# A gated cross-attention stack on one core: in the third and fifth layers the output transposes and the output projection are issued one round later, and in the third the next queries and keys ahead of the scores

## The reference

```python
# third layer ("l1x"): 16 heads of 8, queries from x, keys and values from ctx
q = (query @ Wq.T + bq) * 8 ** -0.5
k, v = key @ Wk.T + bk, key @ Wv.T + bv
scores = einsum('bhtd,bhsd->bhts', qh, kh) + add_mask
out = einsum('bhts,bhsd->bhtd', softmax(scores), vh)
return out @ Wo.T + bo
# fifth layer ("l2x"): RMS norm of x and ctx, 4 query heads of 32 over one key head, rope, mask
q, k = rope(xn @ q_w) * 32 ** -0.5, rope(mn @ kv_w[0])
enc = softmax(where(mask, q @ k.T, MASK_FILL)) @ (mn @ kv_w[1])
return enc @ out_w
```

## Time and profile before

| what | value |
|---|---|
| median of 3 runs (4495.56 to 4502.85) | 4499.69 us |
| the profiled execution's own time | 4495.28 us |
| its span | 4493.3 us |
| TensorE busy | 3848.1 us, 86% of the span |
| VectorE busy | 2983.7 us, 66% |
| ScalarE busy | 1953.3 us, 43% |
| GpSimd busy | 884.4 us, 20% |
| mean granted TensorE clock, as a share of 2.4 GHz | 0.863 |
| chain that ended last | PE 56%, DVE 20%, SPq 8%, issue 8% |
| third layer | about 1376 to 1925 us from the span's start |
| fifth layer | about 2882 to 3255 us |

### The profile page before, as it was taken

One profiled execution on the slowest core, in us unless ns is written; L12 is line 12 of the kernel. 1 busy time (PEld: TensorE's weight loads), 2 busy tenths in 40 slices (PEclk: granted clock), 3 DMA queues, 4 the chain that ended last, 5 costly groups with the idle time before them and its releaser, 6 DMA issues.

```text
span 4493.3 us, 111186 instructions
## 1 busy us (share of the span) xinstructions
PE 3848.1 (86%) x38938; PEld 3008.1 (67%) x38938; DVE 2983.7 (66%) x9018; ACT 1953.3 (43%) x5436; POOL 884.4 (20%) x639
## 2 busy tenths in 40 slices
PE   5999978888886888889999999877845899999965
PEld 4777745555554556589999999755545767777754
DVE  4666657777765777766666666699972266666669
ACT  3666645655552434333333333222212355555521
POOL 1222223333330000010111111100062032222211
PEclk9999977777776767789999999988757999999976
DMA  3000010000001000000000000100004400000000
GB/s 130 8 7 8 7 23 6 6 6 6 6 7 68 15 16 15 14 6 0 0 0 0 0 0 3 43 11 11 8 22 166 147 13 12 12 12 12 10 13 26
DMA packets 102378, 98.15 MB, mean 22 GB/s; under 512 B 31728, under 2 KB 91120, under 8 KB 101616
## 3 DMA queue, kind: packets, MB, share of 16 engines
q1 hardware_dynamic: 97728, 77.99, 5.8%
q0 software_dynamic: 4096, 8.40, 0.6%
q10 hardware_dynamic: 432, 10.19, 0.6%
HBM read 48.02 MB, written 19.66 MB: 15 GB/s over the span
## 4 chain that ended last, share of the span: by engine, by line
PE 56%; DVE 20%; SPq 8%; issue 8%; POOL 3%; DMA 2%; ACT 2%; DVEq 1%; POOLq 0%; ACTq 0%
PE ps L781 52%; SPq L602 7%; PE ps L942 4%; DVE acc L1685 2%; DMA arena_a<-kT 1%; POOL route L753 1%; POOL scr L731 1%; DVE mx L1554 1%; DVE probs L1556 1%; DVE arena_b L1627 1%; DVE st L1417 1%; DVE o_sb L1667 1%; DVE xn L1458 1%; DVE vsmall L1635 1%; DVE mx L1543 1%
## 5 line engine op out<-in xcount | busy, mean ns | idle before, releaser
L781 PE MATMUL ps<-xcT,small 128*128 128x256 f32 x2176 | 618.4, 422 | 54.1 <-DMA xcT<-in_ctxT 27.2
L781 PEld LDWEIGHTS ps<-xcT,small 128*128 128x128 f32 x2176 | 412.4, 204 | 266.9 <-issue 105.5
L1294 ACT ACTIVATE kT<-ps 128x256 f32<-128x256 f32 (+1 forms) x768 | 294.4, 383 | 625.2 <-PE ps L781 549.0
L781 PE MATMUL ps<-arena_b,qT 64*64 64x64 f32 (+3 forms) x11136 | 543.6, 242 | 21.8 <-DVE arena_b L1627 20.4
L745 POOL TENSOR_TENSOR rstd<-veps,neghalf 128x2 f32<-128x2 f32 (+1 forms) x224 | 167.6, 748 | 1959.5 <-DVE veps L1450 1626.1
L759 POOL TENSOR_TENSOR probs<-probs,den 128x1024 f32<-128x1024 f32 x192 | 363.6, 1901 | 936.7 <-DVE den L1574 669.7
L781 PE MATMUL ps<-xhi,parts_a 128*128 128x256 f32 (+1 forms) x2112 | 501.2, 289 | 22.7 <-DVE qT L1714 22.7
L781 PE MATMUL ps<-small,xcT 128*64 128x64 f32 (+5 forms) x3072 | 482.1, 383 | 44.9 <-DVE acc L1685 33.1
L781 PEld LDWEIGHTS ps<-arena_b,qT 64*64 64x64 f32 (+3 forms) x11136 | 463.6, 149 | 59.1 <-issue 36.4
L1266 ACT ACTIVATE pT<-ps 128x512 f32<-128x512 f32 (+1 forms) x576 | 302.1, 571 | 435.6 <-PE ps L942 434.6
L1714 DVE TENSOR_TENSOR qT<-kT,ps 128x256 f32<-128x256 f32 (+1 forms) x768 | 316.5, 419 | 191.3 <-ACT kT L1294 184.0
(11 more groups left out here) (217 smaller groups left out, 7133.3 us busy)
## 6 DMA issues: line engine op xcount, KB each, us to landing
wbuf<-parts_b SPq DMA_DIRECT2D x39, 512.0 KB, 3.0
arena_a<-kT SPq DMA_DIRECT2D x1024, 8.0 KB
xcT<-in_ctxT SPq DMA_DIRECT2D x96, 128.0 KB, 2.1
xn<-scr SPq DMA_DIRECT2D x39, 128.0 KB, 2.2
scr_y<-acc SPq DMA_DIRECT2D x39, 128.0 KB, 2.9
scr<-vsmall SPq DMA_DIRECT2D x9, 512.0 KB, 13.4
ctx_sb<-in_ctx SPq DMA_DIRECT2D x32, 128.0 KB, 2.1
arena_a<-in_w ACTq DMA_DIRECT2D x1, 4096.0 KB, 12.1
```

The costliest lines, as they stand in the source:

```text
L781: return nc.tensor.matmul(o, lhsT, rhs, start=start, stop=stop, skip_group_check=True)
L1294: nc.scalar.activation(silu_buf(k)[0:n, :], bank(b)[0:n, 0:GT], ACT.Silu).then_inc(s_act.sem, 1)
```

## The change

In the third layer `QK` stands ahead of `S0` in the round. In both layers `X0`, `X1`, `W0`, `W1` get a lag of two groups instead of one and stand among the items at the round's start instead of at its end. The numbering of the bank uses is sorted by lag, so that it stays T, A, X, W. The two layers run one round more at their end, in which only the last group's `X` and `W` are left.

```diff
-        for item, lag in order:
+        for item, lag in sorted(order, key=lambda e: -min(e[1], 0)):
             if item[0] in ("L", "M", "H", "S", "P", "N"):
                 continue
             (self.front if lag == 1 else self.body).extend([item] * uses.get(item[0], 1))
...
     l1x = Layer(2, "l1x", stages(
-        "F+ S0 QK+ S1 L++ T0- T1- N0 A0- A1- P0 P1 N1 M++ V+ X0- X1- W0- W1-"),
+        "F+ X0-- QK+ X1-- S0 W0-- S1 L++ W1-- T0- T1- N0 A0- A1- P0 P1 N1 M++ V+"),
         narrow, (6, 7), 16, 8 ** -0.5, True)
...
     l2x = Layer(4, "l2x", stages(
-        "S0 L++ F+ S1 Q+ T0- T1- P0 A0- P1 A1- K+ N0 M++ X0- X1- N1 W0- V+ W1-"),
+        "S0 X0-- X1-- L++ F+ W0-- W1-- S1 Q+ T0- T1- P0 A0- P1 A1- K+ N0 M++ N1 V+"),
         {"T": 1, "A": 1}, (6, 7), 4, 32 ** -0.5, True)
```

## The result

| | before | after |
|---|---|---|
| median of the runs, same job (us) | 4501.27 (4495.56 to 4504.62) | 4726.28 (4719.06 to 4727.77) |
| ratio to before, 95% interval | | 1.0498 (1.048 to 1.0516) |
| span of the profiled execution (us) | 4493.3 | 4725.5 |
| third layer: first line 1540 to last line 1703 (us) | 546.9 | 762.2 |
| fifth layer: line 1387 (the mask, made once) to last line 1540 (us) | 373.5 | 381.9 |

The change makes the kernel 225 us slower; 4761 us was forecast, with 4630 to 4835 as the range. Of the 232 us between the two profiled spans, 215.3 lie in the third layer and 8.4 in the fifth.

A forecast was written before the change was run, and what follows sets the result against it. The prediction took the key-copy loop to bound the third layer and VectorE the fifth. It summed 4495.3 + 251 (third) + 10 (fifth) = 4756 us, 4761 us with 4.4 us to the median; range 4630 to 4835 us.

The forecast's parts named there:

- The copies bind now, VectorE is just under it: Third layer before: the loop S0, QK, eviction, key copies ends last, by about 1 us over VectorE's.
- the second loop: Third layer before: the loop through VectorE, about 15.9 us a round without the copy wait.
- The bank ring: Third layer: T0's second half waits for VectorE's late read of W1; bank 7 back 12.3 us after S0's start.
- T0's second half and T1: Third layer: these transposes and the hand-over to A0, 1.9 us at clock 1.0, 3.6 us at 0.5.
- A0 and A1: Third layer: these 32 matmuls take 3.76 us at clock 1.0, about 6 us at 0.5.
- midway: Third layer: T and A partly at clock 0.5, so a round of 25.0 us, between 23.1 and 27.0.
- The mean clock below 0.70: Sign expected in the profile after: mean granted clock in the third layer's stretch under 0.70.
- The fifth layer: +10, bounds 0 and 46: VectorE-bound layer: nothing gained, 0.3 us a round lost, +10 us, bounds 0 and +46.
- the two lost covers: Fifth layer: `x_sb` update hiding S0's matmuls (wait up to 0.5 us), and A0 ready 0.6 us before VectorE takes it.
- The full clock: Rival, third layer: T, A, QK and S0 all at 1.0, 21.1 us a round, 4631 us; chance 0.09.
- Only the hand-overs: Rival, third layer: bank back in time, 18.9 us a round, 4562 us; chance 0.06.
- Faster: Rival, third layer: copy wait gone, W's result stalls nobody, -1.0 us a round, 4469 us; chance 0.05.

The follow-up runs named there:

- e7: The kernel before, third layer only, with the statistics moved ahead of S0; 4497.95 us, ratio 0.9999.
- e9: The kernel before, third layer only, with three of sixteen key copies issued on ScalarE's queue just ahead of V's eviction; 4461.18 us, ratio 0.992.
- e3: The changed kernel, third layer: VectorE reads W1 right behind W0, ahead of S1's softmax, TensorE's order kept; 4579.66 us, ratio 1.0188.
- e6: The kernel before, third layer only, with three of sixteen key copies issued on ScalarE's queue right behind QK's eviction; 4525.52 us, ratio 1.0054.
- e5: The changed kernel with QK put back behind S0 in the third layer; 4714.65 us, ratio 1.048.
- e2: The fifth layer as changed, the third layer as in the kernel before; 4505.51 us, ratio 1.002.
- e11: The changed kernel, third layer reordered: W0, W1 and the statistics ahead of S0, QK still ahead of S0; 4501.69 us, ratio 1.0008.
- e4: The kernel before with one edit, QK ahead of S0 in the third layer; 4520.96 us, ratio 1.0054.

## Why the prediction was right, and where it was off

**The copies bind now, VectorE is just under it: right.** e7 shows that the second loop doesn't bind (no change, and the copies' wait the same 17.2 us), and e9 that the first does. Without the copies' wait the round was to be about 15.9 us; e9 gives 15.6.

**The bank ring: right, in place and in size.** Bank 7 was to come back 12.3 us after S0's start; 1659.64 to 1671.47 and 0.28 are 12.1 us. TensorE waits there for `acc` of line 1703, 5.2 us, as said. That it is this read and not the order on TensorE is shown by e3, in which the read alone moves and 145 of the third layer's 215 us go. What the prediction didn't name is the first half of that wait: T0's first half also waits, 2.48 us, for W0's bank. By the rows that costs nothing of its own, since T0's second half stands behind the later bank anyway.

**T0's second half and T1**: 1.9 to 3.6 us, 2.75 in the sum; 2.7 measured (1648.02 to 1650.73), at clock 0.50 and with three quarters of the transposes in it.

**A0 and A1: the term that was mis-sized.** "I expect T and A partly at 0.5: 25.0 us, midway" put A at 4.9 us. It took 4.05, since the clock is back at 1.00 from about 1651.4 us on, 0.7 us into A. That is 0.8 us of the 1.2 us by which the round is shorter than the forecast. The rest is A1's division and the normalisation with 1.45 us for 1.6 (1654.78 to 1656.23), the head F to S0 with 3.41 for 3.5, and the bank with 0.2. 1.2 us in 31 rounds are 37 us, and 251 less 215 is 36. The fault is in "midway": in this kernel A has two lengths, 4.0 and 7.0 us, and hardly one between, so that a round is 23.8 or 26 to 27 us and a value in the middle is the one that doesn't occur. (That is no rule: in e6 A takes lengths from 5.5 to 6.7 us.) Nothing in the prediction's rows said which of the two A would take in most rounds; the range held both, so the time would have fallen inside it either way. The price at the lower clock was too low as well, about 6 us where it needs 7.0. The prediction's own row gives more than it took: 0.8 us for the last four are 0.2 us each, 6.4 us for 32. With 7.0 the midway value would have been 25.5 us and the miss larger, so the two faults partly cancelled. With all else as in the sum that puts a round at 28 us, where the slow ones took up to 27.1.

The Trainium skill ("TensorE: Matmul & The Clock Gate", section "HAM oscillation — how this bites in real kernels") has the group of matmuls behind a long wait start at the lower clock; the prediction took T and A together for that group. The trace agrees for the transposes (0.50 from 1648.02 us on) and not for A, which followed without a gap and ran at 1.00 from 0.7 us in. In three of the early rounds, and in most of e5's, where the same wait of 5.2 us stands ahead of the same work, A did run at 0.50.

The prediction also had the rows of the kernel before agree with that rule, since S0 behind its wait runs at 0.5. They don't bear on it. S0's wait is 1.03 us, and the clock was down long before it. TensorE in the kernel before, while A ends, V runs and the first transpose of `o_sb` starts:

```profile
1623.20:1624.40 1.20, 1.20 (x22) 1.00 0.06 14
1624.40:1624.80 0.40, 0.40 (x9) 0.61 0.09 21
```

It fell from 1.00 to 0.50 between 1624.4 and 1624.8 us, with TensorE busy throughout these stretches, and stayed there through the next QK. A long wait is thus not the only thing ahead of a fall.

**The mean clock below 0.70**: it is 0.69 over the layer, as good as before, and 0.72 in the round shown. TensorE's work grew little and the clock stands at each level for about the same share of a longer round; as a sign of the mechanism it was worth nothing.

**VectorE idle some 5 us before line 1663 and as much before line 1540**: 4.6 and 5.6 us. Right. The layer was to take some 800 us and took 762.2.

**The fifth layer: +10, bounds 0 and 46.** 8.4 us in the changed kernel, 9.1 in e2. The first of the two lost covers shows. VectorE's waits from 3168 to 3418 us of the kernel after, the stretch that answers to the earlier trace rows:

```profile
DVE probs L1540 <- PE ps L781: 3.9, 10, 0.4
```

The first scores come late by up to 0.4 us in about every second round, where no such wait stood before. The second cover isn't lost: no wait before line 1663 is listed. 3.9 us in 250 are 5.8 in the layer; the rest, some 3 us, is no more than what the fifth layer scatters where no edit touches it (370.7 to 373.5 us).

**The rivals.** The full clock (4631 us): no, the head and the transposes run at 0.50. Only the hand-overs (4562 us): it needed the bank in time, which the changed order doesn't give; e3 comes near to it by that very means, with 4580 us, 2 us of wait a round left and A at the lower clock in a third of its rounds. Faster (4469 us): it was to be decided by whether W1 is read within 5.8 us of S0, and it was read after 11.8. Even with the bank in time (e11) the third layer gains 10 us and not 31, so that rival was wrong in its price as well: it took out the copies' wait and forgot that QK then stands on the path to the scores, 24 us in e4.

## What to carry to other kernels

When an item is moved to a later round, follow the buffer it holds, and not only its data: who gives the buffer back, what stands ahead of that instruction on its engine, and which engine queues behind it. Here a wait that closed a ring between two engines, each of which walks its list in order, turned overlap into taking turns, and each of them showed idle time that looked like the other's fault: the read of one 0.3 us result, behind another tile's softmax and the statistics, cost 145 us. And before work is pulled ahead to hide a transfer, see whether the transfer can be made shorter at its source: three of sixteen issues on another queue, at the point where that engine is idle, gave the 1.2 us a round that the reordering was after, and the same three issues 6 us earlier cost 27 us instead of gaining 38, for the most part by way of the clock at which A then ran. And where a stage has been seen at two clocks, price both ends and don't forecast the middle.

## What the runs showed of the hardware that was not expected

- Thirty-two matmuls of 128x36 took 3.76 us at a granted clock of 1.00 (before) and 6.98 us at 0.50 (e5), a factor of 1.86.
- In the kernel before the granted clock fell from 1.00 to 0.50 at 1624.4 to 1624.8 us with TensorE busy for all of these 0.4 us and of the 1.2 us ahead.
- After the same wait of 5.2 us and the same transposes at 0.50, the granted clock rose 0.7 us into A in most rounds of the changed kernel, and not during A in most rounds of e5. These two kernels stay at one of the two for many rounds in a row, 2.5 to 3 us a round apart; e3 changes between them every few rounds, and e6 has lengths of A in between (5.5 to 6.7 us).
- Three DMA issues of 8 KB hold ScalarE's queue for 1.97 us (e6), and SyncE's takes 10.67 us for sixteen (before): 0.66 and 0.67 us each, the same on both. In e6 the first eviction of the transposes starts at 1648.99 us, behind the last issue: on an engine that also computes, issues are work.
